# Attention maps: the row of maxima turned one slot earlier, and a burst of matmuls every 86 slots instead of every 22

## The reference

```
q = q.reshape(B, N, H, 2, HD); k = k.reshape(B, N, H, 2, HD); v = v.reshape(B, N, H, 2 * HD)
s = jnp.einsum('bnhd,bmhd->bhnm', qi, ki) * scale        # for each of the two maps
p = jax.nn.softmax(s, axis=-1)
a = jnp.einsum('bhnm,bmhe->bhne', p, v)
o = a1 - lam * a2
```

## Time and profile before

| | |
|---|---|
| runs | 3350.38, 3353.21, 3379.68 us; median 3353.21 |
| profiled execution | 3336.01 us; its span 3334.0 us |
| TensorE busy | 2880.8 us (86% of the span) |
| VectorE busy | 2460.6 us (74%) |
| ScalarE busy | 2119.2 us (64%) |
| mean granted TensorE clock | 0.947 |
| attention maps | from 107.4 to 833.2 us |

### The profile page before, as it was taken

One profiled execution on the slowest core, in us unless ns is written; L12 is line 12 of the kernel. 1 busy time (PEld: TensorE's weight loads), 2 busy tenths in 40 slices (PEclk: granted clock), 3 DMA queues, 4 the chain that ended last, 5 costly groups with the idle time before them and its releaser, 6 DMA issues. The chain is left out here.

```text
span 3334.0 us, 71750 instructions
## 1 busy us (share of the span) xinstructions
PE 2880.8 (86%) x27397; PEld 1718.8 (52%) x27428; DVE 2460.6 (74%) x3103; ACT 2119.2 (64%) x3079; POOL 1309.5 (39%) x923
## 2 busy tenths in 40 slices
PE   5899999999668888888888888888888889779997
PEld 3222222222545565555555555555655555558886
DVE  3888887784258787878787878787878787656564
ACT  2587787777137687878787777777778777511111
POOL 1000000000057575757575757575757575400000
PEclk7799999998579999999999999999999999989998
DMA  3010110010010001000100010001000000000001
GB/s 133 21 26 24 26 27 24 25 27 8 2 58 8 7 8 39 8 6 9 41 7 7 7 41 8 6 9 39 8 7 7 20 9 5 5 26 0 0 0 32
DMA packets 56466, 64.37 MB, mean 19 GB/s; under 512 B 24742, under 2 KB 38964, under 8 KB 55348
## 3 DMA queue, kind: packets, MB, share of 16 engines
q1 hardware_dynamic: 55380, 60.58, 6.7%
q10 hardware_dynamic: 864, 0.79, 0.1%
HBM read 36.69 MB, written 7.34 MB: 13 GB/s over the span
## 5 line engine op out<-in xcount | busy, mean ns | idle before, releaser
L883 DVE TENSOR_REDUCE a_minus_max<-a_ps_max 128x1 f32<-128x1024 f32 x512 | 597.2, 1219 | 130.3 <-PE a_ps_max L810 125.3
L793 ACT ACTIVATE a_expT<-a_ps_scoresT 128x512 f32<-128x512 f32 (+1 forms) x683 | 533.7, 810 | 178.6 <-PE a_ps_scoresT L828 169.6
L1175 POOL TENSOR_TENSOR b_turned_q<-b_rot_q,b_turned_q 128x1024 f32<-128x1024 f32 x96 | 227.4, 2369 | 378.7 <-DVE b_turned_q L1538 378.7
L843 PE MATMUL a_ps_out<-a_expT,v_aug 128*32 128x256 f32 x4096 | 340.2, 405 | 4.7 <-ACT a_outT L780 4.2
L1446 PE MATMUL b_psD<-b_w_qkv,b_xs 128*128 (+1 forms) x384 | 216.0, 650 | 129.3 <-ACT b_outT L1286 129.3
L1273 ACT ACTIVATE b_kT<-b_psD 64x512 f32<-64x512 f32 x384 | 227.1, 591 | 130.2 <-PE b_psD L1363 123.2
L764 POOL CAST a_max_hi<-a_minus_max 128x16 bf16<-128x16 f32 x32 | 6.3, 196 | 703.4 <-DVE a_minus_max L883 703.4
L1607 DVE STREAM_TRANSPOSE b_probsT<-b_probs 32x512 f32<-32x512 f32 x384 | 265.6, 692 | 9.0
L828 PE MATMUL a_ps_scoresT<-a_q_op,a_k_op 26*128 26x512 bf16 x1024 | 248.3, 399 | 25.1 <-ACT a_max_rows L774 16.9
L1402 PE MATMUL b_psS<-b_kT,b_qT 128*32 128x128 f32 x6144 | 207.5, 276 | 55.6 <-ACT b_kT L1273 49.6
L1215 POOL TENSOR_TENSOR b_probs<-b_probs,b_inv_sum 128x1024 f32<-128x1024 f32 x96 | 182.6, 1902 | 183.6 <-DVE b_inv_sum L1583 183.6
(11 more groups left out here) (296 smaller groups left out, 5954.2 us busy)
## 6 DMA issues: line engine op xcount, KB each, us to landing
b_v_edge<-b_v SPq DMA_DIRECT2D x96, 128.0 KB
b_w_qkv<-L_ffn_Wqkv SPq DMA_DIRECT2D x6, 1536.0 KB
a_q_op<-terms_q SPq DMA_DIRECT2D x128, 48.0 KB
a_k_op<-terms_k SPq DMA_DIRECT2D x128, 48.0 KB
joined<-a_outT SPq DMA_DIRECT2D x256, 16.0 KB
b_w_o<-L_ffn_Wo SPq DMA_DIRECT2D x6, 512.0 KB
a_q_op<-a_max_rows SPq DMA_DIRECT2D x128, 4.0 KB
b_w<-L_ffn_W SPq DMA_DIRECT2D x6, 341.0 KB
```

The costliest lines, as they stand in the source:

```text
L793: act.activation(expT[:, to:to + 512 * size], ps_scoresT[:, at:at + 512 * size], ACT.Exp, scale=SCALE_A).then_inc(exp_ready, 1)
L843: last_mm = pe.matmul(ps_out[lo:lo + 32, 256 * part:256 * part + 256], v_aug[:, b * T8 + kt, head, :], expT[:, at:at + 256], start=(kt == ...
L883: dve.tensor_reduce(minus_max[p % 2][:, side, 0, qt:qt + 1], ps_max[u % 2][:], AX.X, ALU.max, negate=True).then_inc(max_taken, 1)
L1175: pool.tensor_tensor(turned[:], rot[:], turned[:], ALU.add).then_inc(added, 1)
```

## The change

Two things change, both in `attention_maps`. The bursts stand in `range(8, 683, 86)`: slots 8, 94, 180, 266, 352, 438, 524 and 610. And the turn of a row is issued at the end of the slot ahead, behind that slot's scores and its weighing part, after a wait for the exponential of slot e - 2, which is the last to read the bank of `ps_row`; ScalarE copies the row in front of the exponential of that slot ahead, no longer in front of the exponential of the turn's own slot. The wait of TensorE for the copy (`row_held`) stays where it was, ahead of the scores that overwrite the bank.

```diff
-        WARM_SLOTS = range(8, EXPS, 22)
+        WARM_SLOTS = range(8, EXPS, 86)
...
-                if e in turn_at:
-                    row_copy(turn_at[e])
+                if e + 1 in turn_at:
+                    row_copy(turn_at[e + 1])
                 act.wait_ge(scoresT_ready, end)
...
                 if e in WARM_SLOTS:
                     warm()
                 if e in turn_at:
-                    turn_row(turn_at[e])
                     pe.wait_ge(row_held, turn_at[e] + 1)
                 scores(e)
                 if e in part_at:
                     weigh(part_at[e])
+                if e + 1 in turn_at:
+                    pe.wait_ge(exp_ready, e)
+                    turn_row(turn_at[e + 1])
```

## The result

The kernel became faster: 3261.9 us median (3255.1 to 3272.3, four runs) against 3351.8 us (3343.3 to 3379.7, four runs); the ratio is 0.972, 95% interval 0.966 to 0.978. The profiled execution took 3262.9 us (span 3260.8), 73.1 us less than the one before.

The account below looks back on a forecast made before the run. Only TensorE's order and clock were taken to set the attention maps' time. 33 + 35.5 + 12 - 12 = 68.5 us off the profiled 3336.0 gave 3267.5; 5 added made 3273 us, range 3252 to 3325.

Parts of the forecast that it names:

- Bursts (33 us): Attention maps: 23 of 31 bursts go; 18 fewer at full clock save 1.84 us each, 33 us.
- Low stretches (35.5 us): After the first burst: five stretches at 1.2 GHz, 68.3 us in all, vanish; 35.5 us saved, their five bursts included.
- Turns (12 us): The 31 row turns, issued a slot earlier, get cheaper: 3 + 9 = 12 us saved.
- The first kind: The 20 turns in slots with e % 4 = 3: 0.15 us saved each, 3 us in all.
- The second: The 11 turns in slots with e % 4 = 1: 0.81 us saved each, 8.9 us in all.
- ScalarE's new wait for the transpose: Sign of being right: ScalarE waits about 0.3 to 0.5 us at L817, thirty-one times.
- The other signs: 56 or so recorded burst matmuls, no TensorE wait over 0.5 us for the copy, clock 1.00 until the last turn.
- The tail (12 us lost): Behind the last turn, slot 653, the clock falls to the stage's end: 11 us plus 1; slightly likelier than not.
- The 5 us for the distance between profile and median: Added because the median of runs lay 17 us above the profiled execution; the gap might go or stay.
- the steady fall without cover: Rival: the plain four-slot cycle does not hold the clock between the fewer bursts; about 3480 us, chance 0.05.
- The dangerous rival: The clock falls behind the same turns as now, slots 205, 397, 461, 525, until the next burst; 3431 us, chance 0.07.

Follow-up runs that it names:

- the turn alone: New kernel with a burst every 22 slots as before, so only the turn is changed against the kernel before: 3298.6 us, ratio 0.981.
- one kind of old turn: New kernel with the 11 turns of e % 4 = 1 in their old place, 3400.2 us; with the 20 of e % 4 = 3, 3266.0 us.
- the bare hole: New kernel plus 11 waits of TensorE for an exponential, in e % 4 = 1 slots without a turn: 3492.2 us, ratio 1.045.
- the bursts alone: Kernel before with only its bursts thinned to every 86 slots, turn in its old place: 3432.6 us, ratio 1.015.

## Why the prediction was right

The forecast was faster, 3273 us, range 3252 to 3325; measured 3261.9.

1. **Bursts (33 us).** Right. 1.84 us each at full clock, and nothing catches up: 42.6 us for 23 of them in the kernel with the turn alone.
2. **Low stretches (35.5 us).** Right: all five are gone. That they hang on the turn's hole, which I had read from where they began, the kernels with one kind of old turn and the bare hole show. For the stretch in the tail this is weaker, since there the clock also fell without such a hole.
3. **Turns (12 us).** The sum is right, 20 x (0.74 - 0.50) + 11 x (1.25 - 0.60) = 12 us, but by luck: its two terms are off in opposite ways. The first kind gained 0.24 us, not 0.15: I let the exponential start 0.30 us behind the copy's start, measured 0.17. The second gained 0.65, not 0.81: I put exponential 334 only 0.62 us behind 333, but TensorE has the unit of maxima of slot 334 ahead of its scores, and the exponential had 0.31 us to wait for them. Also, ScalarE's new wait for the transpose is not 0.3 to 0.5 us but 0.51 (second kind) and 0.77 (first kind) where no burst stands ahead. My own chain gives as much: exponential 353 ends at 475.32 and the copy was to start at 476.07, and 331 ends at 452.35 and the copy at 452.82. The other signs came as named: 56 recorded matmuls of bursts, one wait of 0.4 us for the copy, and the clock at 1.00.
4. **The tail (12 us lost).** Held to be slightly likelier than not, and it did not happen in the profiled execution. This is the step that is off: without it the sum is 80.5 us, and the stage gained 81.3. It was the right price for a real event: in six traces that reached the tail at full clock with all turns of the second kind new and no bare hole, the clock fell there twice (slots 652 and 666), at 11.4 us in the first. The chance was put too high by these six, which are few.
5. **The 5 us for the distance between profile and median.** Wrong: the new median lies 1 us below its profile. The prediction had the reason among its two: the executions of the kernel before differ in low clock. Of seven taken beside the first experiments, the four of 3344 to 3352 us had a mean clock of 0.944 to 0.946, the three of 3369 to 3379 us one of 0.932 to 0.936. With the low stretches that distance went.

Of the rivals, the steady fall without cover is refuted by the single burst that lasted 619 us. It had its rule from the Trainium skill ("TensorE: Matmul & The Clock Gate", "A second HAM failure mode: psum-queue depth-cycling"), by which small idles between groups, as the banks go round, make the clock swing. The trace does not agree for the full cycle: banks go round in every slot, and at either level the clock stands still until a larger hole or a burst comes. In the tail it might apply: the fall in slot 666 had nothing longer than holes of 0.33 us ahead of it. The same page of the Trainium skill warns, in the table of "Why this matters for your kernels", of idle gaps of TensorE several times as long as the 0.86 and 0.97 us that were enough here, in work in which TensorE otherwise read as idle for 3% of the time (18.7 of 618.7 us with one burst).

The dangerous rival was real, only not for this kernel: the bursts alone give 3432.6 us. I gave it 0.07 on the ground that the second kind's hole shrinks, and that is the very thing that separates the two kernels.

## What to carry to other kernels

Before removing work that holds TensorE's clock (the cover, here the bursts), find where each low stretch begins and what stands there: it may be one short wait, and once that is gone nearly all of the cover is pure cost. Do the two together, and in that order: thinning the cover alone turned stretches of 3 to 20 us into ones of 36 to 130 us. And a stage can sit at either level with the same instructions, so where a single short burst must raise the clock, leave it a margin: with four matmuls in it one of two executions missed, at 370 us.

## What the runs showed of the hardware

- The stage has two lasting levels. With the same cycle it ran 619 us at 2.4 GHz behind one burst, and 1011 us at 1.2 GHz without one.
- A single hole of 0.81 to 0.97 us among dense work, at full clock, was often enough for a fall (the last of the 11 in each kernel stands in the tail and is longer, 1.08 or 1.19 us, and was followed by a fall each time): in 5 of 11 cases in the kernel before, 5 of 9 with fewer bursts, 6 of 10 with only these turns old, 7 of 8 with bare waits, one trace each. One of 0.36 us was not, in 53 cases at full clock (20, 13 and 20 in three kernels). Why one hole of 0.86 us takes and the next does not, no run here shows.
- In the tail, where TensorE has less work, the clock fell behind shorter holes: once behind one of 0.45 us and once behind one of 0.33 us, in six traces.
- Whether a burst of four matmuls raises the clock differs between executions of one kernel (3619.2 and 3249.8 us). Eight in slot 8 did in all eight traces that had them; eight in slot 2 in none of four executions (mean clock 0.822 to 0.825).
